# Three pair buffers, and channel halves for the first pair, in the opening statistics of a two-layer similarity kernel

## The chip, the cores and the metric

The kernel runs on one core of one Trainium2 chip. The metric is the device time of one execution in microseconds (us). Work is spread over five engines that run on their own and meet at semaphores: TensorE (PE, whose weight loads are shown as PEld), VectorE (DVE), ScalarE (ACT), GpSimd (POOL) and SyncE (SP), which here only issues transfers to the core's 16 DMA engines.

## The reference, cut to what matters

The input has the shape 2 x 256 x 256 x 384 (images, rows, columns, channels) in float32. Two equal layers run one after the other, each a group normalisation followed by a ratio of box sums that is added to the layer's input:

```python
def _gn(v, G=32, eps=1e-5):              # 12 channels in a group
    g = v.reshape(B_, H_, W_, G, C_ // G)
    m = jnp.mean(g, axis=(1, 2, 4), keepdims=True)
    s = jnp.var(g, axis=(1, 2, 4), keepdims=True)
    return ((g - m) / jnp.sqrt(s + eps)).reshape(v.shape)
# conv_ref(x), box sums of width 5 along W and 20 along C:
s = box_sum(x, 2, 5);  num = box_sum(s * s, 3, 20)
d = box_sum(box_sum(x * x, 2, 5), 3, 20)
ratio = nan_to_num(num / (d * norm), nan=1.0)
x = x + _L0_conv_ref(_gn(x))
x = x + _L1_conv_ref(_gn(x))
```

A mean and a variance of a group are taken over a whole image. So nothing of an image can be normalised before all of that image has been read once.

## The kernel before

The work has four phases, (layer, image) = (0, 0), (0, 1), (1, 0), (1, 1). An image has 32 tiles (`TILES`) of 8 rows; a tile is 3072 KB, in SBUF 128 partitions x 16 segments (`SEGS`) x 384 channels. In a phase TensorE forms the width sums and the channel sums for one pair of image rows after another, and the other engines centre, square, divide and add around it.

Ahead of phase 0 stands the opening: VectorE has to measure all 32 tiles of image 0, and no other engine has work meanwhile. The statistics of the other images are measured beside the phases, as a third user of VectorE's time (`measure_beside`, `measure_output`), and the change leaves them as they are.

In the opening two tiles are measured at a time, as a pair j of 0 to 15. `measure` issues 32 `bn_stats`, one for each group, over both tiles of the pair. A pair lies in `x_both` (even j) or `y_both` (odd j); each of its two tiles is loaded by a transfer of its own with its own semaphore (`in_landed[0..3]`). SyncE's program (`measure_loads`, L225) issues the four loads of pairs 0 and 1 at once. Then, for each pair that `tile_measured` counts as done, it issues the two loads of the pair that comes two later. So pair j + 2 can't be asked for before pair j is measured, and while pair j is being measured only pair j + 1 is on its way.

These loads take the image in an order in which a partition's part of a tile is one stretch of 24,576 bytes (16 x 384 x 4), which is allowed since a mean doesn't ask for an order. The last pair, 15, is loaded otherwise (L231): by channel halves. One transfer brings channels 0 to 191 of both tiles, the other the rest, in rows of 768 bytes (192 x 4), and VectorE measures 16 groups, sums them up, and does the same for the other 16. When pair 7 is measured, `opening_totals` (L643) sums up the first half of the image with 32 `bn_aggr`.

When pair 14 is measured, SyncE also issues the loads of the first two tiles of phase 0 (L237), in rows of 1,536 bytes. Behind the last `bn_aggr` come the short chain `ask_means` and `finish` (L680 to L723: VectorE and TensorE by turns, ScalarE for a logarithm and an exponential), and then the phases. `loads_before` tells POOL how many loads had gone into `x_both` before a phase.

Of the kernel before, what the change touches and what calls it, by code (L numbers as in the profile page):

```python
# [29 lines left out]
P = 128  # L30
# [21 lines left out]
def similarity_layers_kernel(nc, x, out):  # L52
# [9 lines left out]
    LAYERS = 2  # L62
    PHASES = [(layer, b) for layer in range(LAYERS) for b in range(B)]
    NP_ = len(PHASES)
    assert W == 2 * P and C == 3 * P and TILES % 4 == 0 and B == 2 and TILES >= 8

    SPLIT = TILES // 2
    CUT = GROUPS // 2
# [4 lines left out]
    BESIDE = TILES - UPFRONT  # L73
    BESIDE_SPLIT = (SPLIT - UPFRONT) // 2
    BESIDE_END = BESIDE // 2
    REACH = W_BOX // 2
    WN = P + REACH
    HALF_COL = [0, P - REACH]
# [12 lines left out]
    with ExitStack() as ctx:  # L91
        def sb(name, shape, dt=F32):
            return ctx.enter_context(nc.sbuf_tensor(name, shape, dt))
# [5 lines left out]
        y_both = sb("y_both", [P, 2 * SEGS, C])  # L99
        x_in = [x_both[:, i * SEGS:(i + 1) * SEGS, :] for i in range(2)]  # L100
        y_out = [y_both[:, i * SEGS:(i + 1) * SEGS, :] for i in range(2)]
        stat_tiles = [x_in[0], x_in[1], y_out[0], y_out[1]]
        stat_pairs = [x_both, y_both]
        centred = [sb(f"centred{i}", [P, PSEG, C]) for i in range(2)]
        square = [sb(f"square{i}", [P, PSEG, C]) for i in range(2)]
        sT = [sb(f"sT{i}", [P, KB, 2 * W]) for i in range(2)]
        tT = [sb(f"tT{i}", [P, KB, 2 * W]) for i in range(2)]
        recip = [sb(f"recip{i}", [P, PSEG, C]) for i in range(2)]
        with nc.sbuf_tensor("beside", [P, SEGS, C], F32) as beside:
            pass  # L110
        top = [sb(f"top{i}", [P, KB, 2 * W], BF16) for i in range(2)]
# [28 lines left out]

        in_landed = [sem(f"in_landed{i}") for i in range(4)]
        out_landed = [sem(f"out_landed{i}") for i in range(2)]
        ones_set = sem("ones_set")
        bands_cut = sem("bands_cut")
        bands_ready = sem("bands_ready")
# [64 lines left out]
        with nc.Block() as block:  # L210

            @block.sync
            def _(sp):

                view = tiles_of(x, 0)
                runs = x[0].rearrange("h w c -> (h w) c").rearrange("(t p s) c -> p t s c", p=P, s=SEGS)

                def measure_loads(i, lo):
                    for s in range(4):
                        if lo > 0 and s % 2 == 0:  # L220

                            sp.wait_ge(tile_measured, i * 2 + s // 2 - 1)
                        if lo == TILES // 4 - 1 and s >= 2:
                            continue
                        sp.dma_start(stat_tiles[s][:].unsqueeze(1), runs[:, bass.ds(i * 4 + s, 1), :, :]  # L225
                                     ).then_inc(in_landed[s], 16)
                looped(sp, TILES // 4, measure_loads, [0, TILES // 4 - 1])

                for part in range(2):
                    cs = slice(part * CUT * CG, (part + 1) * CUT * CG)  # L230
                    sp.dma_start(y_both[:, :, cs], view[:, (TILES - 2) * SEGS:TILES * SEGS, cs]  # L231
                                 ).then_inc(in_landed[2 + part], 16)

                for s in range(2):

                    sp.wait_ge(tile_measured, TILES // 2 - 1)
                    sp.dma_start(x_in[s][:], tiles_of(x, 0)[:, s * SEGS:(s + 1) * SEGS, :]  # L237
                                 ).then_inc(in_landed[s], 16)
                def load_beside(n):

                    sp.dma_start(beside[:], tiles_of(x, 1)[:, bass.ds((UPFRONT + n) * SEGS, SEGS), :]
                                 ).then_inc(beside_landed, 16)


                for s in range(UPFRONT):

                    sp.wait_ge(means_asked, 1)
                    sp.dma_start(y_out[s][:], tiles_of(x, 1)[:, s * SEGS:(s + 1) * SEGS, :]
                                 ).then_inc(in_landed[2 + s], 16)
                    if s == 0:  # L250
                        load_beside(0)

                sp.wait_ge(beside_done, 3)
                load_beside(1)
                for ph, (layer, b) in enumerate(PHASES):
                    src = tiles_of(source[layer], b)
                    dst = tiles_of(target[layer], b)
                    bodies = TILES // 2

                    def move_tiles(i, lo):  # L260
                        last = lo == bodies - 1
                        for s in range(2):
                            m = i * 2 + s
                            if last and s == 1 and ph == NP_ - 1:

                                for g in range(PAIRS):
                                    sp.wait_ge(rows_out, pairs_before(ph) + m * PAIRS + g + 1)
                                    sp.dma_start(dst[:, m * SEGS + g * PSEG:m * SEGS + (g + 1) * PSEG, :],
                                                 y_out[1][:, g * PSEG:(g + 1) * PSEG, :]
                                                 ).then_inc(out_landed[1], 16)  # L270
                                continue

                            sp.wait_ge(rows_out, pairs_before(ph) + (m + 1) * PAIRS)
                            if not last:
                                sp.dma_start(x_in[s][:], src[:, bass.ds((m + 2) * SEGS, SEGS), :]
                                             ).then_inc(in_landed[s], 16)
                            elif ph + 1 < NP_:
                                nl, nb = PHASES[ph + 1]
                                if nl > 0:

                                    for o in range(2):
                                        sp.wait_ge(out_landed[o], 16 * (TILES // 2) * (nb + 1))
                                sp.dma_start(x_in[s][:], tiles_of(source[nl], nb)[:, s * SEGS:(s + 1) * SEGS, :]
                                             ).then_inc(in_landed[s], 16)
                            sp.dma_start(dst[:, bass.ds(m * SEGS, SEGS), :], y_out[s][:]
                                         ).then_inc(out_landed[s], 16)
                            if ph == 0 and lo < BESIDE_END - 1:

                                sp.wait_ge(beside_done, (m + 2) * 3)
                                load_beside(m + 2)  # L290
                    looped(sp, bodies, move_tiles, [bodies - 1], [(BESIDE_END - 1, None)] if ph == 0 else [])

                for s in range(2):
                    sp.wait_ge(out_landed[s], 16 * ((TILES // 2) * NP_ + s * (PAIRS - 1)))


            def loads_before(ph):
                return TILES // 4 + ph * (TILES // 2)

            @block.gpsimd  # L300
            def _(pool):
# [303 lines left out]
            def _(dve):  # L605
# [38 lines left out]
                    link(last)  # L644


                def measure_two(base, i, s):

                    for o in range(2):
                        dve.wait_ge(in_landed[2 * s + o], (base + i + 1) * 16)  # L650
                    measure(stat_pairs[s], range(GROUPS), out_stats, i * 2 + s).then_inc(tile_measured, 1)

                for half in range(2):
                    with dve.Fori(0, SPLIT // 4 - half) as i:
                        for s in range(2):
                            measure_two(half * (SPLIT // 4), i, s)
                    if half == 0:
                        dve.wait_ge(tile_measured, SPLIT // 2)
                        opening_totals(0, range(GROUPS))

                measure_two(SPLIT // 4, SPLIT // 4 - 1, 0)
                for part in range(2):
                    groups = range(part * CUT, (part + 1) * CUT)
                    dve.wait_ge(in_landed[2 + part], TILES // 4 * 16)
                    link(measure(y_both, groups, out_stats, SPLIT // 2 - 1))
                    if part == 0:
                        dve.wait_ge(tile_measured, TILES // 2 - 1)
                    opening_totals(1, groups)


                dve.wait_ge(bands_cut, 2 * HALVES + KB + 1)
                for d in range(REACH):
# [92 lines left out]
                def measure_output(ph, i, lo, e, part):  # L765
# [6 lines left out]
                    if ph == 0 and lo == 0 and early:  # L772

                        if q == 0 or part == 0:
                            return
                        if q == 1:
                            dve.wait_ge(in_landed[3], (TILES // 4 + 1) * 16)

                        last = measure(y_out[1], range((q - 1) * chunk, GROUPS if q == 3 else q * chunk),
                                       beside_stats, 1)  # L780
                        if q == 3:
                            link(last)
                        return
# [57 lines left out]
                ask_means(0)  # L841
                finish(0)

                dve.wait_ge(in_landed[2], (TILES // 4 + 1) * 16)
                measure(y_out[0], range(GROUPS), beside_stats, 0).then_inc(tile_measured, 1)
                dve.wait_ge(tile_measured, TILES // 2)
                for ph in range(NP_):
# [49 lines left out]
```

## Time and profile before

| | us |
|---|---|
| median of three runs | 5876.69 |
| lowest and highest of the three | 5875.77, 5883.06 |
| the profiled execution's own time | 5877.14 |
| its span in the trace | 5875.4 |
| busy in the span: PE, PEld | 5516.0, 5489.9 |
| busy in the span: DVE, POOL, ACT | 4830.5, 4585.6, 4491.6 |

The span reaches from the first instruction of the program to the last one's end. Busy time of an engine is the union of its instructions' times. The granted clock of TensorE was 0.998 of its full speed in this execution. In the rows below a start is counted from the start of the span, and "idle before" is the time in which the engine did nothing, with the event that ended it.

### The profile page before, as it was taken

The page shows a single profiled execution, that of the slowest core. Times are in us where ns is not written, and L with a number is a line of the kernel's source. Part 1 is how long each engine was busy: PE and PEld are TensorE (multiplying, and loading weights), DVE is VectorE, ACT ScalarE, POOL GpSimd, SP SyncE. Part 2 cuts the span into 40 slices and gives each one's busy share as a digit, 9 for nine tenths or more (in the row PEclk, how much of TensorE's full clock was granted, in tenths as well). Part 3 has the DMA queues.
Part 4 walks back from the last instruction along what each step waited for, and adds up shares of the span by engine and source line. Part 5 has one row for each costly group of instructions (what it writes and reads, how often), then busy time and mean ns, then how long its engine had stood idle before and what let it go on. Part 6 is the DMA issues. An engine that isn't in the chain of part 4 may idle for free.

```text
span 5875.4 us, 145274 instructions
## 1 busy us (share of the span) xinstructions
PE 5516.0 (94%) x53804; PEld 5489.9 (93%) x53804; DVE 4830.5 (82%) x8140; ACT 4491.6 (76%) x6153; POOL 4585.6 (78%) x1427
## 2 busy tenths in 40 slices
PE   0099999999999999999999999999999999999999
PEld 0099999999999999999999999999999999999999
DVE  8988889988889999999999777777777777777776
ACT  0077777777877788878887788888888888888887
POOL 0056665566658899889998899999999999999998
PEclk9999999999999999999999999999999999999999
DMA  9965655566633444434344343444444443434343
GB/s 383 348 212 201 225 204 204 196 206 223 207 136 129 146 155 141 159 129 162 138 157 144 129 161 138 156 143 152 148 147 153 143 157 138 162 132 168 129 171 129
DMA packets 607136, 1007.81 MB, mean 172 GB/s; under 512 B 5168, under 2 KB 603184, under 8 KB 603184
## 3 DMA queue, kind: packets, MB, share of 16 engines
q1 hardware_dynamic: 607024, 1006.65, 48.1%
q14 instruction: 83, 0.68, 0.0%
q8 instruction: 29, 0.48, 0.0%
HBM read 603.98 MB, written 402.65 MB: 171 GB/s over the span
## 4 chain that ended last, share of the span: by engine, by line
PE 67%; DVE 4%; ACT 0%; issue 0%; POOLq 0%; POOL 0%; DVEq 0%; ACTq 0%
PE width_ps L527 35%; PE num_ps L555 18%; PE den_ps L564 14%; DVE recip L742 1%; DVE y_both L753 1%; DVE lane_mv L637 1%; DVE den_ps L735 1%; DVE out_stats L630 1%; PE den_ps L555 0%; DVE mid L728 0%; ACT recip L449 0%; DVE stat_two L684 0%; DVE beside_stats L630 0%; ACT top L430 0%; ACT recip L442 0%
## 5 line engine op out<-in xcount | busy, mean ns | idle before, releaser
L344 POOL TENSOR_TENSOR centred<-x_both,mean_row 128x1536 f32<-128x1536 f32 x512 | 1773.6, 3464 | 983.0 <-PE width_ps L527 690.4
L555 PE MATMUL num_ps<-band_c,sT 128*128 128x138 f32 (+2 forms) x12288 | 1811.6, 284 | 29.6 <-DVE y_both L753 29.2
L353 POOL TENSOR_TENSOR y_both<-x_both,y_both 128x1536 f32<-128x1536 f32 x512 | 1776.2, 3469 | 17.5 <-DVE y_both L753 17.5
L527 PE MATMUL width_ps<-band_wc,square 128*128 128x130 f32 x12288 | 1651.6, 277 | 17.0 <-DVE mid L728 12.5
L555 PEld LDWEIGHTS num_ps<-band_c,sT 128*128 128x128 f32 x12288 | 1609.0, 190 | 38.2 <-DVE y_both L753 13.6
L527 PE MATMUL width_ps<-band_w,centred 128*128 128x130 f32 x12288 | 1562.5, 276 | 0.0
L527 PEld LDWEIGHTS width_ps<-band_wc,square 128*128 128x128 f32 x12288 | 1507.1, 191 | 19.9 <-DVE mid L728 10.1
L527 PEld LDWEIGHTS width_ps<-band_w,centred 128*128 128x128 f32 x12288 | 1459.8, 191 | 0.4
L442 ACT ACTIVATE recip<-den_ps,bias_ln 128x768 f32<-128x768 f32 x1024 | 920.2, 899 | 644.8 <-PE den_ps L564 450.0
L735 DVE SCALAR_TENSOR_TENSOR den_ps<-den_ps,recip 128x768 f32<-128x768 f32 x1024 | 987.2, 964 | 499.2 <-ACT recip L449 472.6
L361 POOL TENSOR_TENSOR low<-mid 128x1536 bf16<-128x1536 f32 x384 | 1055.2, 2748 | 282.9 <-DVE mid L728 282.9
L433 ACT ACTIVATE sT<-width_ps,rstd_col 128x512 f32<-128x512 f32 x1536 | 1056.4, 688 | 208.9 <-PE width_ps L527 208.7
L728 DVE SCALAR_TENSOR_TENSOR mid<-width_ps,rvar_col,top 128x512 f32<-128x512 f32 x1152 | 860.9, 747 | 385.0 <-ACT top L430 383.9
L753 DVE SCALAR_TENSOR_TENSOR y_both<-num_ps,recip 128x768 f32<-128x768 f32 x1024 | 976.6, 954 | 67.1 <-DVE recip L742 2.0
L742 DVE SCALAR_TENSOR_TENSOR recip<-den_ps,recip 128x768 f32<-128x768 f32 x1024 | 974.5, 952 | 18.7
L449 ACT ACTIVATE recip<-recip,bias_exp 128x768 f32<-128x768 f32 x1024 | 952.6, 930 | 0.1
L430 ACT ACTIVATE top<-width_ps,rvar_col 128x512 bf16<-128x512 f32 x1152 | 791.8, 687 | 164.6 <-PE width_ps L527 110.7
L414 ACT ACTIVATE square<-centred 128x768 f32<-128x768 f32 x1024 | 853.9, 834 | 1.9 <-POOL centred L344 1.9
L564 PE MATMUL den_ps<-band_b,mid 128*128 128x138 bf16 (+2 forms) x4608 | 725.9, 225 | 0.0
L564 PE MATMUL den_ps<-band_b,top 128*128 128x138 bf16 (+2 forms) x4608 | 725.6, 225 | 0.0
L630 DVE BATCH_NORM_STATS2 out_stats<-y_both 128x192 f32 (+2 forms) x2304 | 696.4, 367 | 7.3 <-DMA y_both<-in_x_dram 6.8
L564 PE MATMUL den_ps<-band_b,low 128*128 128x138 bf16 (+2 forms) x4608 | 534.5, 225 | 0.0
(55 smaller groups left out, 2877.3 us busy)
## 6 DMA issues: line engine op xcount, KB each, us to landing
x_both<-in_x_dram SPq DMA_DIRECT2D x80, 3072.0 KB, 11.0
first_layer_out<-y_both SPq DMA_DIRECT2D x64, 3072.0 KB, 18.3
x_both<-first_layer_out SPq DMA_DIRECT2D x64, 3072.0 KB, 10.9
out_dram<-y_both SPq DMA_DIRECT2D x63, 3072.0 KB, 18.1
beside<-in_x_dram SPq DMA_DIRECT2D x30, 3072.0 KB, 10.9
y_both<-in_x_dram SPq DMA_DIRECT2D x18, 3072.0 KB, 16.8
out_dram<-y_both SPq DMA_DIRECT2D x4, 768.0 KB, 3.6
```

The lines of the kernel that those rows point to most:

```text
L344: nc.gpsimd.tensor_tensor(centred[e % 2][:], x_in[slot][:, g * PSEG:(g + 1) * PSEG, :], mean_row[ph % 2][:].unsqueeze(1).to_broadcast([P, ...
L353: nc.gpsimd.tensor_tensor(y_out[slot][:, g * PSEG:(g + 1) * PSEG, :], x_in[slot][:, g * PSEG:(g + 1) * PSEG, :], y_out[slot][:, g * PSEG:( ...
L361: nc.gpsimd.tensor_tensor(low[par][:], mid[par][:], top_half(mid[par]), ALU.subtract).then_inc(low_cut, 1)
L433: nc.scalar.activation(sT[par][:, k, :], src, ACT.Square, scale=rstd_col[ph][:, k:k + 1]).then_inc(width_taken, 1)
L442: nc.scalar.activation(recip[par][:, 2 * h:2 * h + 2, :], den_ps[h][:, :, 0:C], ACT.Ln, bias=bias_ln[:], scale=LN_SCALE).then_inc(log_done, 1)
L449: nc.scalar.activation(both, both, ACT.Exp, bias=bias_exp[:], scale=-1.0).then_inc(recip_done, 1)
L527: last = nc.tensor.matmul(bank[:, at:at + WN], data[:, r * 2 + j, P * k:P * (k + 1)], band[:, j, :], start=(r == 0 and j == 0), stop=(r == ...
L555: last = nc.tensor.matmul(bank[:, lo:hi], data[:, k, at:at + P], band_c[k][:], start=(k == 0), stop=(k == KB - 1), skip_group_check=True)
L564: last = nc.tensor.matmul(bank[:, lo:hi], thirds[n][:, k, at:at + P], band_b[k][:], start=(n == 0 and k == 0), stop=(n == 2 and k == KB - ...
L735: nc.vector.scalar_tensor_tensor(near, near, TINY, recip[par][:, 2 * h:2 * h + 2, :], ALU.add, ALU.mult).then_inc(near_done, 1)
L742: nc.vector.scalar_tensor_tensor(both, den_ps[h][:, :, 0:C], 2.0, both, ALU.subtract, ALU.mult).then_inc(den_used, 1)
L753: nc.vector.scalar_tensor_tensor(y_out[slot][:, at:at + 2, :], num_ps[:, :, 0:C], TINY, recip[e % 2][:, 2 * h:2 * h + 2, :], ALU.add, ALU.mult
```

## The change

The opening statistics use three buffers of two tiles, in turn: pair j goes into buffer j % 3 of `y_both`, `spare_pair`, `x_both`. `spare_pair` is a new name for memory that is otherwise idle in the opening: it lies where `centred`, `square`, `sT` and `tT` are later, 49,152 bytes of each partition, and ends where they end. SyncE issues the loads of pairs 0, 1 and 2 at once and those of pair j when pair j - 3 is measured. Pair 0 is loaded and measured by channel halves, as the last pair already was. Pair 14 still lies in `x_both` and pair 15 in `y_both`. The loops of the opening on SyncE and on VectorE are written out in full, and the counts that later waits compare with are adapted (`X_USES` 5, `Y_USES` 6).

```diff
+    X_USES = (TILES // 2 - 1) // 3
+    Y_USES = X_USES + 1
...
-        stat_tiles = [x_in[0], x_in[1], y_out[0], y_out[1]]
-        stat_pairs = [x_both, y_both]
+        with nc.sbuf_tensor("spare_pair", [P, 2 * SEGS, C], F32) as spare_pair:
+            pass
...
+        stat_pairs = [y_both, spare_pair, x_both]
...
+        spare_landed = [sem(f"spare_landed{i}") for i in range(2)]
+        stat_landed = [in_landed[2:4], spare_landed, in_landed[0:2]]
...
-                def measure_loads(i, lo):
-                    for s in range(4):
-                        if lo > 0 and s % 2 == 0:
-
-                            sp.wait_ge(tile_measured, i * 2 + s // 2 - 1)
...
+                for j in range(TILES // 2):
+                    if j >= 3:
+
+                        sp.wait_ge(tile_measured, j - 2)
+                    for part in range(2):
+                        if j in (0, TILES // 2 - 1):
+                            cs = slice(part * CUT * CG, (part + 1) * CUT * CG)
+                            sp.dma_start(stat_pairs[j % 3][:, :, cs], view[:, j * 2 * SEGS:(j + 1) * 2 * SEGS, cs]
+                                         ).then_inc(stat_landed[j % 3][part], 16)
+                        else:
+                            m = j * 2 + part
+                            sp.dma_start(stat_pairs[j % 3][:, part * SEGS:(part + 1) * SEGS, :].unsqueeze(1),
+                                         runs[:, m:m + 1, :, :]).then_inc(stat_landed[j % 3][part], 16)
...
-                return TILES // 4 + ph * (TILES // 2)
+                return X_USES + ph * (TILES // 2)
...
+                def measure_halves(j):
+
+                    for part in range(2):
+                        groups = range(part * CUT, (part + 1) * CUT)
+                        dve.wait_ge(stat_landed[j % 3][part], (j // 3 + 1) * 16)
+                        last = measure(stat_pairs[j % 3], groups, out_stats, j % (SPLIT // 2))
+                        if j == TILES // 2 - 1:
+                            link(last)
+                            if part == 0:
+                                dve.wait_ge(tile_measured, TILES // 2 - 1)
+                            opening_totals(1, groups)
+                    return last
+
+                measure_halves(0).then_inc(tile_measured, 1)
+                for j in range(1, TILES // 2 - 1):
+                    for part in range(2):
+                        dve.wait_ge(stat_landed[j % 3][part], (j // 3 + 1) * 16)
+                    measure(stat_pairs[j % 3], range(GROUPS), out_stats, j % (SPLIT // 2)).then_inc(tile_measured, 1)
+                    if j == SPLIT // 2 - 1:
+                        dve.wait_ge(tile_measured, SPLIT // 2)
+                        opening_totals(0, range(GROUPS))
+                measure_halves(TILES // 2 - 1)
```

On SyncE, at the start of its program, this stood before, with the loop that the branch closes:

```order
L225 DMA x_both<-in_x_dram 128x6144 x2
L225 DMA y_both<-in_x_dram 128x6144 x2
L201 UNCONDITIONAL_BRANCH
L201 ISA
L225 ISA [waits tile_measured]
L225 DMA x_both<-in_x_dram 128x6144
L225 ISA
L225 DMA x_both<-in_x_dram 128x6144
L225 ISA [waits tile_measured]
L225 DMA y_both<-in_x_dram 128x6144
```

And this stands at the same place of SyncE's program of the changed kernel:

```order
L230 DMA y_both<-in_x_dram 128x32x192 x2
L234 DMA spare_pair<-in_x_dram 128x6144 x2
L234 DMA x_both<-in_x_dram 128x6144 x2
L234 DMA y_both<-in_x_dram 128x6144 [waits tile_measured]
L234 DMA y_both<-in_x_dram 128x6144
L234 DMA spare_pair<-in_x_dram 128x6144 [waits tile_measured]
```

Six loads now stand ahead of the first wait in place of four, and the first two of them are the halves of pair 0, which are in rows of 192 channels.

On VectorE, behind the fourteen `memset` of its program, each `bn_stats` of a looped pair had a register instruction (ISA) of its own before. A piece of it, at the end of pair 0's and the start of pair 1's:

```order
L630 ISA
L630 BN_STATS out_stats<-x_both 128x6
L630 ISA [waits in_landed3,in_landed2]
L630 BN_STATS out_stats<-y_both 128x6
L630 ISA
```

The same stretch of VectorE's program of the changed kernel, from pair 0 to pair 3:

```order
L633 BN_STATS out_stats<-y_both 128x6 [waits in_landed2]
L633 BN_STATS out_stats<-y_both 128x6 x15
L633 BN_STATS out_stats<-y_both 128x6 [waits in_landed3]
L633 BN_STATS out_stats<-y_both 128x6 x15
L633 BN_STATS out_stats<-spare_pair 128x6 [waits spare_landed1,spare_landed0]
L633 BN_STATS out_stats<-spare_pair 128x6 x31
L633 BN_STATS out_stats<-x_both 128x6 [waits in_landed1,in_landed0]
L633 BN_STATS out_stats<-x_both 128x6 x31
```

The first 16 `bn_stats` now wait for one half alone and the next 16 for the other, there are as many of them as before, and the register instructions are gone.

## Rows read from the trace of the kernel before

**Rows 1.** The page's slices: busy tenths of an engine in 40 equal slices

```profile
PE   0099999999999999999999999999999999999999
DVE  8988889988889999999999777777777777777776
```

**Rows 2.** Waits in the opening: who waited for whom, us, times, longest

```profile
PE den_ps L499 <- DVE stat_two L684: 291.2, 1, 291.2
DVE out_stats L630 <- DMA x_both<-in_x_dram: 28.6, 7, 16.2
DVE out_stats L630 <- DMA y_both<-in_x_dram: 6.8, 5, 1.7
```

**Rows 3.** VectorE's timeline, opening: start, us, line, form, idle before

```profile
18.53 14.81 DVE L630 BATCH_NORM_STATS2 out_stats<-x_both 128x384 f32 x32 [16.24 <-DMA x_both<-in_x_dram]
33.30 14.81 DVE L630 BATCH_NORM_STATS2 out_stats<-y_both 128x384 f32 x32
51.37 14.81 DVE L630 BATCH_NORM_STATS2 out_stats<-x_both 128x384 f32 x32 [3.26 <-DMA x_both<-in_x_dram]
67.22 14.81 DVE L630 BATCH_NORM_STATS2 out_stats<-y_both 128x384 f32 x32 [1.05 <-DMA y_both<-in_x_dram]
...
147.53 7.51 DVE L643 BATCH_NORM_AGGREGATE lane_mv<-out_stats 128x2 f32<-128x48 f32 x32
155.45 14.81 DVE L630 BATCH_NORM_STATS2 out_stats<-x_both 128x384 f32 x32 [0.42 <-DVE lane_mv L643]
...
267.49 7.44 DVE L630 BATCH_NORM_STATS2 out_stats<-y_both 128x6 f32<-128x384 f32 x16
...
286.31 3.82 DVE L643 BATCH_NORM_AGGREGATE lane_mv<-out_stats 128x2 f32<-128x48 f32 x16
290.17 0.34 DVE L674 TENSOR_SCALAR band_wc<-band_w 128x1 f32<-128x1 f32 x4
```

**Rows 4.** SyncE's loads issued at 0.8 to 2.2: issue, then landing

```profile
L225 SPq DMA_DIRECT2D x_both<-in_x_dram x2: 402/412/421, 0.8 to 1.3; - x2
DMA to landing us min/median/max: 10.2/13.6/17.0
...
L225 SPq DMA_DIRECT2D y_both<-in_x_dram x2: 424/499/574, 1.7 to 2.2; - x2
DMA to landing us min/median/max: 23.9/27.4/30.9
```

**Rows 5.** The same for the loads issued at 33.5 and at 48.3

```profile
L225 SPq DMA_DIRECT2D x_both<-in_x_dram x2: 338/343/348, 33.5 to 34.1; - x2
DMA to landing us min/median/max: 10.3/13.7/17.1
...
L225 SPq DMA_DIRECT2D y_both<-in_x_dram x2: 332/332/333, 48.3 to 48.8; - x2
DMA to landing us min/median/max: 11.4/14.8/18.2
```

**Rows 6.** The same for L231, pair 15's halves in rows of 768 bytes

```profile
L231 SPq DMA_DIRECT2D y_both<-in_x_dram x2: 383/3962/7541, 251.5 to 252.0; - x2
DMA to landing us min/median/max: 13.0/17.6/22.2
```

**Rows 7.** The same for L237, phase 0's tiles in rows of 1,536 bytes

```profile
L237 SPq DMA_DIRECT2D x_both<-in_x_dram x2: 1433/3555/5677, 267.6 to 269.1; - x2
DMA to landing us min/median/max: 15.0/18.4/21.8
```

**Rows 8.** Windows: stretch, busy us of engines, granted clock, DMA share, GB/s

```profile
5.00:10.00 5.00, 0.00 (x0) 0.00 (x0) 0.00 (x0) 0.00 (x0) 1.70 (x6) 1.00 1.03 442
10.00:18.00 8.00, 0.00 (x0) 0.00 (x0) 0.00 (x0) 0.00 (x0) 0.00 (x0) 1.00 0.99 427
51.00:98.00 47.00, 0.00 (x0) 0.00 (x0) 43.81 (x95) 0.00 (x0) 0.00 (x0) 1.00 0.95 395
```

**Rows 9.** Line L707 in all phases: duration ns min, median, max

```profile
L707 DVE TENSOR_SCALAR stat_tmp<-stat_tmp x4: 180/182/2627, 294.4 to 3333.6; 128x32 f32<-128x32 f32 x4
```

More of the change, by code:

```diff
@@ L64, in similarity_layers_kernel @@
     NP_ = len(PHASES)
-    assert W == 2 * P and C == 3 * P and TILES % 4 == 0 and B == 2 and TILES >= 8
+    assert W == 2 * P and C == 3 * P and TILES // 2 % 3 == 1 and B == 2 and TILES >= 8
     SPLIT = TILES // 2
@@ L216, in _ @@
                 runs = x[0].rearrange("h w c -> (h w) c").rearrange("(t p s) c -> p t s c", p=P, s=SEGS)
-                def measure_loads(i, lo):
-                    for s in range(4):
-                        if lo > 0 and s % 2 == 0:
-                            sp.wait_ge(tile_measured, i * 2 + s // 2 - 1)
[L223 to L232, printed above, removed]
+                for j in range(TILES // 2):
[10 more added lines that the diff above has]
+                                         runs[:, m:m + 1, :, :]).then_inc(stat_landed[j % 3][part], 16)
                 for s in range(2):
@@ L644, in opening_totals @@
                     link(last)
[L647 to L657, printed above, removed]
+                def measure_halves(j):
[15 more added lines that the diff above has]
+                    if j == SPLIT // 2 - 1:
                         dve.wait_ge(tile_measured, SPLIT // 2)
                         opening_totals(0, range(GROUPS))
[L661 to L668, printed above, removed]
+                measure_halves(TILES // 2 - 1)
                 dve.wait_ge(bands_cut, 2 * HALVES + KB + 1)
@@ L776, in measure_output @@
                         if q == 1:
-                            dve.wait_ge(in_landed[3], (TILES // 4 + 1) * 16)
+                            dve.wait_ge(in_landed[3], (Y_USES + 1) * 16)
                         last = measure(y_out[1], range((q - 1) * chunk, GROUPS if q == 3 else q * chunk),
@@ L842, in _ @@
                 finish(0)
-                dve.wait_ge(in_landed[2], (TILES // 4 + 1) * 16)
+                dve.wait_ge(in_landed[2], (Y_USES + 1) * 16)
                 measure(y_out[0], range(GROUPS), beside_stats, 0).then_inc(tile_measured, 1)
```

## The prediction

> **What bounds the kernel now.** First the page's slices [rows 1]: TensorE is at 9 tenths or more in 38 slices and idle in the first two. From the start of phase 0 on TensorE sets the pace and VectorE has room; in the opening it is the other way round. The waits say what TensorE stands for there: 291.2 us for `stat_two`, the first thing that VectorE makes from the finished statistics [rows 2]. Nothing else runs meanwhile, so a microsecond saved before 290.17, where the last `bn_aggr` has ended [rows 3], starts everything behind it a microsecond earlier.
>
> VectorE's timeline shows what fills these 290 us [rows 3]. From 18.53 to 33.30 it measures a pair without a pause: 14.77 us. Sixteen pairs make 236.3 us. The sums after pair 7 take 155.45 - 147.53 = 7.9 us, those at the end some 2 x 3.8. Together 251.8. The rest is waiting for loads: 28.6 + 6.8 = 35.4 us in twelve waits [rows 2]. 16.2 of them are the wait for the first pair; 19.2 stand between pairs, 3.26 ahead of pair 2, 1.05 ahead of pair 3, and so on.
>
> Why does it wait between pairs, if the transfers are fast enough? The landings tell. The four loads issued at 0.8 to 2.2 land at 11.0, 18.3, 25.6 and 33.1 [rows 4]. So a load into an idle queue takes 10.2 us, and each one queued behind it only 7.3 to 7.5 more. The first thus has some 10.2 - 7.3 = 2.9 us of start. Two queued loads, a pair, need 14.6 to 14.8 us, which is VectorE's own 14.77. But the loads issued at 33.5 found the queue empty since 33.1 and landed at 43.8 and 51.2 [rows 5]: 18 us for a pair. The next, issued at 48.3, when the queue had 2.9 us of work left, landed at 59.7 and 67.0 [rows 5]: 8.5 + 7.3 = 15.8 us after 51.2. The queue runs nearly dry once in every pair, because the next pair may be asked for only when VectorE has finished one. From 51 to 98 us the transfers move 395 GB/s, from 5 to 18 us, with the queue full, 442 and 427 [rows 8].
>
> **The change, part by part.**
>
> Third buffer. The loads of pair j + 3 are issued when pair j is measured; then pairs j + 1 and j + 2 are landed, moving or queued. The queue does not run dry. I take 14.7 us for a pair, from the loads queued deep [rows 4]. The bounds are 14.6 and the 15.8 of a shallow queue [rows 5].
>
> Pair 0 by halves. The half loads of pair 15 show the price: issued at 251.5 and 252.0, landed at 264.5 and 274.2 [rows 6]. That is 9.7 us for a half (of both tiles, again 3072 KB) in place of 7.3. The first half goes into an idle queue at 0.8 and should land at 0.8 + 2.9 + 9.7 = 13.4, the second at 23.1. VectorE begins 0.2 after a landing (18.53 against 18.3), measures 16 groups in 7.4 us from 13.6 to 21.0, waits, and measures the others from 23.3 to 30.7. Before, pair 0 was done at 33.30. Issuing the second half holds SyncE for 7.5 us [rows 6], so the loads of pairs 1 and 2 are issued at about 9 to 11; the queue has work until 23.1, so this costs nothing.
>
> Now the price: pair 1 is behind these slower halves. Its tiles land at 30.4 and 37.8, and VectorE starts it at 38.0 where before it started at 33.30. Starting early buys nothing that is kept, since pair 1 is 4.7 us later. Pair 2 lands at 37.8 + 14.7 = 52.5 and is started at 52.8, against 51.37 before. Until here the change is 1.4 us behind.
>
> The Trainium skill (DMA: Bandwidth & Descriptors, Specifications) puts the size from which a transfer runs at line rate at 512 B, so 768 bytes would cost what 24,576 do. Pair 1 would then land at 0.8 + 2.9 + 4 x 7.3 = 32.9, and the gain be 4.9 us larger. The trace disagrees with its 9.7 against 7.3, though with other loads ahead and behind it; the row is taken, and 7.3 is its lower bound.
>
> From pair 1 on. VectorE needs 14.77 a pair and the queue 14.7, so VectorE sets the pace, barely. Pairs 1 to 7 end at 38.0 + 7 x 14.77 = 141.4. The 7.9 of sums bring it to 149.3, and in this time the loads get ahead by as much. Pairs 8 to 14 end at 252.7. The tail from the start of pair 15 to 290.17 was 290.17 - 267.49 = 22.7 [rows 3] with both halves there in time; now they are asked for one pair earlier and the queue has more to spare. So the statistics end at 275.4 in place of 290.17: **14.8 us earlier**.
>
> What else moves. There are as many `bn_stats` and `bn_aggr` as before. The register instructions of the loops go; they cost nothing, as pairs measured in the loop follow one another in 14.77 and the straight-line half of pair 15 takes 7.44 [rows 3]. The loads of phase 0's first two tiles leave, as before, when pair 14 is measured, 22.7 us ahead of the end, and took 15.0 and 21.8 to land [rows 7] while pair 15's second half was still moving; now nothing is moving, so they are no later. `spare_pair` is last used by pair 13, and the first write into `centred` waits for the means anyway. Behind 290 us the instructions and buffers are the same.
>
> The sum: 5877.14 - 14.8 = 5862.3 for the profiled execution. Its own time is 0.4 above the median of the three runs, by which it would be 5861.9. I say **5862.0**. A measurement of this kernel can tell about 0.2% from no change, 11.8 us, so the gain is 3 us above that bound.
>
> **The rivals.**
>
> *The shallow queue's price stays.* The 8.5 us between 51.2 and 59.7 [rows 5] could be a price of each new issue and not of its lateness. For it: it is so wherever a pair is asked for in the middle of another's transfer. Against it: the third load at the start was issued 16.6 us ahead of its turn and landed 7.3 after the second [rows 4]. Then pair j lands at 37.8 + 15.8 (j - 1), pair 7 at 132.6; its measuring and the sums end at 155.5; pair 8 is there by then, and so is each pair up to 14 (243.2, against 244.1 on VectorE), which ends at 258.9. Plus 22.7 makes 281.6, a gain of 8.6: 5868.5. Chance 0.12.
>
> *Straight code stalls.* One instruction of VectorE's stands out: L707 took 2627 ns once, in the opening, and some 182 otherwise [rows 9]. The trace does not say why; it may have waited for its code. The change writes 512 `bn_stats` out, each run once, and shifts all of VectorE's later code. Each such stall in the opening costs 2.4 us, with nothing to hide it; two to four make 5867 to 5872. On the other side L707's own may vanish, which would give up to 2 us more. Against it: the straight-line parts around 267.49 show no such pause. Chance 0.08.
>
> *The rate falls under a full queue, slower than before.* The opening is then bound by transfers from end to end. The point from which this decides: before, pair 14 was started 14.77 before 267.49, at 252.7. If its load lands later than 252.5, the change loses. That is (252.5 - 23.1) / 14 = 16.4 us a pair, or 6.29 MB (2 x 3072 KB) / 16.4 = 384 GB/s. The nearest rows are those of L237: 282.6 and 290.9, so 8.3 for a tile in rows of 1,536 bytes [rows 7]. At 16.6 a pair, pair 14 lands at 255.5 and the opening ends 3 us later than before: 5880. It takes 17.2 a pair to be slower by 0.2%. Against it stand the 442 and 427 GB/s, though over 13 us only [rows 8]. Chance 0.05.
>
> The Trainium skill (DMA: Bandwidth & Descriptors, Where 436 GB/s comes from) has a rule for this rival: between HBM and SBUF the HBM side binds at about 358 GB/s a core. At that rate, an estimate from this page, a pair takes 17.6 us and the time would be some 5894. The trace already moves 395 over 47 us with pauses in it, so I give the rule no more than that chance.
>
> *Something behind the opening gives the gain back*, a shifted load or loop: I see no place for it, chance 0.05.
>
> **How the numbers follow.** The forecast has 0.70, with a range of its own of 5857 (halves at 7.3) to 5865 (pairs at 15.0 in place of 14.7 for the first seven, 2 us, and 1 us of scatter). The shallow queue reaches to 5868.5 and two stalls to 5867. I take 5857 to 5870; about 1.5 in 10 is outside. Faster by over 0.2%, below 5864.9: nearly all of the forecast's 0.70 and a little of stalls with one stall only, 0.72. Within 0.2%: the shallow queue, most of the stalls, half of the falling rate and most of what gives the gain back, 0.24. Slower by over 0.2%: 0.04.
>
> **What the profile of the changed kernel would show.** VectorE's first `bn_stats` at 13.6, a wait of some 2 us ahead of the second half, a long one of about 7 ahead of pair 1 to 38, and then waits of under 0.3 us for each pair; pair 2 at about 52.8, and the last `bn_aggr` ended at 275.4. Loads of 24,576-byte stretches land 7.3 to 7.5 after one another across pairs too. Where they land 8.5 apart at each new pair, the first rival is right. Pauses inside a pair, with its load long landed, would be the stalls. TensorE's first wait should be 276.4, and its waits behind it unchanged. The prediction is wrong if the rate across pairs is not that of the first four loads, or if the halves of pair 0 do not take 9.7 at the start, where VectorE is idle.

## The result, and the profile after

| | median us | runs | ratio to before, 95% interval |
|---|---|---|---|
| before | 5877.02 | 10 | |
| changed | 5863.55 | 10 | 0.9976, 0.9968 to 0.9985 |

The change makes the kernel 13.5 us faster, 0.23%. The forecast was 5862.0, in a range of 5857 to 5870. One of the ten runs of the changed kernel, 20152 us at a granted clock of 0.444 of full speed, is left out of the ratio.

The profiled execution has a span of 5863.4 us, 12.0 under that of before. The page, and the waits of its opening:

```profile
span 5863.4 us, 144735 instructions
...
PE 5512.5 (94%) x53804; PEld 5486.7 (94%) x53804; DVE 4830.7 (82%) x8140; ACT 4491.7 (77%) x6153; POOL 4585.5 (78%) x1427
```

```profile
PE den_ps L502 <- DVE stat_two L686: 275.7, 1, 275.7
...
DVE out_stats L633 <- DMA y_both<-in_x_dram: 13.6, 3, 11.0
DVE out_stats L633 <- DMA spare_pair<-in_x_dram: 7.2, 1, 7.2
...
DVE out_stats L633 <- DMA x_both<-in_x_dram: 0.2, 1, 0.2
```

TensorE now waits 275.7 us for the statistics in place of 291.2 [rows 2]. VectorE's waits for loads are 13.6 + 7.2 + 0.2 = 21.0 in place of 35.4, and they lie elsewhere. VectorE's timeline in the opening, which answers to [rows 3]:

```profile
13.25 7.46 DVE L633 BATCH_NORM_STATS2 out_stats<-y_both 128x6 f32<-128x384 f32 x16 [10.96 <-DMA y_both<-in_x_dram]
22.86 7.45 DVE L633 BATCH_NORM_STATS2 out_stats<-y_both 128x6 f32<-128x384 f32 x16 [2.16 <-DMA y_both<-in_x_dram]
37.55 14.81 DVE L633 BATCH_NORM_STATS2 out_stats<-spare_pair 128x6 f32<-128x384 f32 x32 [7.24 <-DMA spare_pair<-in_x_dram]
52.51 14.81 DVE L633 BATCH_NORM_STATS2 out_stats<-x_both 128x6 f32<-128x384 f32 x32 [0.15 <-DMA x_both<-in_x_dram]
67.23 14.79 DVE L633 BATCH_NORM_STATS2 out_stats<-y_both 128x6 f32<-128x384 f32 x32
...
111.92 14.81 DVE L633 BATCH_NORM_STATS2 out_stats<-y_both 128x6 f32<-128x384 f32 x32 [0.48 <-DMA y_both<-in_x_dram]
...
141.47 7.51 DVE L646 BATCH_NORM_AGGREGATE lane_mv<-out_stats 128x2 f32<-128x48 f32 x32
...
251.97 7.44 DVE L633 BATCH_NORM_STATS2 out_stats<-y_both 128x6 f32<-128x384 f32 x16
...
274.65 0.34 DVE L676 TENSOR_SCALAR band_wc<-band_w 128x1 f32<-128x1 f32 x4
```

Three waits at the start (10.96, 2.16, 7.24), then one of 0.15 and one of 0.48. The statistics end at 274.65, 15.5 us before 290.17. The landings of pair 0's halves, and the transfer rate (stretch, busy us, clock, DMA share, GB/s) in the window behind them:

```profile
L230 SPq DMA_DIRECT2D y_both<-in_x_dram x1: 436/436/436, 0.8 to 0.8; - x1
DMA to landing us min/median/max: 12.4/12.4/12.4
...
L230 SPq DMA_DIRECT2D y_both<-in_x_dram x1: 7163/7163/7163, 1.3 to 1.3; - x1
DMA to landing us min/median/max: 21.5/21.5/21.5
```

```profile
24.00:105.00 81.00, 0.00 (x0) 0.00 (x0) 73.61 (x161) 0.00 (x0) 0.00 (x0) 1.00 1.00 430
105.00:220.00 115.00, 0.00 (x0) 0.00 (x0) 114.45 (x266) 0.00 (x0) 0.00 (x0) 1.00 1.00 430
```

The halves land at 13.2 and 22.8, 9.6 us apart. Behind them the queue moves 430 GB/s for nearly 200 us without a gap, where it moved 395 between 51 and 98 before [rows 8]. This is the whole of the change's work, and it did what it says.

But 15.5 us were won in the opening and 12.0 arrive at the end of this execution. The sums of `beside_stats`, all in phase 0, mark where the rest goes; their first and last start, in the kernel before and in the changed one:

```profile
L637 DVE BATCH_NORM_AGGREGATE lane_mv<-beside_stats x64: 528/530/574, 903.5 to 1696.5; 128x2 f32<-128x96 f32 x64
```

```profile
L640 DVE BATCH_NORM_AGGREGATE lane_mv<-beside_stats x64: 526/529/577, 885.4 to 1684.8; 128x2 f32<-128x96 f32 x64
```

At 903.5 the changed kernel is 18.1 us ahead, 2.6 more than at the opening's end. At 1696.5 it is 11.7 ahead. So 6.4 us are lost between the two, and there is no edit there. VectorE's waits ended by "issue" (the engine waited for nothing that the view shows), the whole of them, before and after:

```profile
DVE beside_stats L630 <- issue: 13.6, 8, 1.8
```

```profile
DVE beside_stats L633 <- issue: 7.2, 4, 1.9
DVE den_ps L737 <- issue: 5.1, 4, 1.4
```

Before, 8 pauses of 1.7 us; after, 4 of 1.8 and 4 of 1.3, the latter at a place where there was none. One of them, in VectorE's timeline of the changed kernel:

```profile
1384.71 1.13 DVE L633 BATCH_NORM_STATS2 out_stats<-y_both 128x192 f32 x4
1387.42 0.88 DVE L633 BATCH_NORM_STATS2 beside_stats<-beside 128x192 f32 x3 [1.58 <-issue]
1389.71 0.97 DVE L737 SCALAR_TENSOR_TENSOR den_ps<-den_ps,recip 128x768 f32<-128x768 f32 x1 [1.41 <-issue]
```

The first is at the start of a round of a loop (8 pairs of image rows), the second a few instructions on. Phase 0 has two such loops on VectorE, of four or five rounds. In the trace before, four pauses lie in rounds of the first loop (between 300 and 850 us) and four in those of the second (between 1130 and 1550). In the changed kernel the first loop has none and the second has all eight. That asks for a cause, and the experiments have two threads: what each half of the change is worth, and what makes these pauses.

### The profile page after: what moved, and what is told of

The parts are those of the page before. It is cut to its first block, busy times and chain, and to the rows that moved or that the text cites. A ratio compares the mean times of both kernels' runs of the same rounds, so it can differ in the third digit from the quotient of the medians.

```text
span 5863.4 us, 144735 instructions
## 1 busy us (share of the span) xinstructions
PE 5512.5 (94%) x53804; PEld 5486.7 (94%) x53804; DVE 4830.7 (82%) x8140; ACT 4491.7 (77%) x6153; POOL 4585.5 (78%) x1427
## 4 chain that ended last, share of the span: by engine, by line
PE 67%; DVE 4%; issue 0%; ACT 0%; POOLq 0%; POOL 0%; DVEq 0%; ACTq 0%
PE width_ps L530 35%; PE num_ps L558 18%; PE den_ps L567 14%; DVE recip L744 1%; DVE y_both L755 1%; DVE lane_mv L640 1%; DVE den_ps L737 1%; DVE out_stats L633 1%; PE den_ps L558 0%; DVE mid L730 0%; ACT recip L452 0%; DVE beside_stats L633 0%; ACT top L433 0%; ACT recip L445 0%; DVE stat_two L686 0%
## 5 line engine op out<-in xcount | busy, mean ns | idle before, releaser
L737 DVE SCALAR_TENSOR_TENSOR den_ps<-den_ps,recip 128x768 f32<-128x768 f32 x1024 | 987.4, 964 | 507.7 <-ACT recip L452 475.9
L633 DVE BATCH_NORM_STATS2 out_stats<-y_both 128x192 f32 (+2 forms) x2240 | 666.8, 362 | 14.1 <-DMA y_both<-in_x_dram 13.6
```

The lines of the kernel that those rows point to most:

```text
L737: nc.vector.scalar_tensor_tensor(near, near, TINY, recip[par][:, 2 * h:2 * h + 2, :], ALU.add, ALU.mult).then_inc(near_done, 1)
```

## The experiments

Two theories on the opening. **Queue**: the gain comes from the queue that never runs dry, and the halves of pair 0 cost more than they bring, since pair 1 stands behind them. **Early start**: the halves bring the gain. Two on the pauses. **Place** (A): where a loop stands in VectorE's program decides. **Moment** (B): the phases start at another moment of the loads. The change writes out VectorE's opening, and all later instructions stand 191 places further on (counted in the built programs, before they are compiled).

### The third buffer alone

```diff
-                        if j in (0, TILES // 2 - 1):
+                        if j == TILES // 2 - 1:
...
-                measure_halves(0).then_inc(tile_measured, 1)
-                for j in range(1, TILES // 2 - 1):
+                for j in range(TILES // 2 - 1):
```

> The changed kernel with three buffers, but pair 0 loaded as two whole tiles in stretches of 24,576 bytes and measured at once, as the pairs behind it. Theory of the prediction (a transfer queue that never runs dry, 7.3 us a tile, and halves of 9.6): pair 0 lands at 18.3 and is measured from 18.5, pair 1 lands at 33.0 and is measured from 33.3 in place of 37.55, all else follows at 14.7 a pair, and the last sums end at about 270.4, 4.2 us before those of the changed kernel (274.6). Time about 5859.5. Rival (the halves are what gives the gain, by starting VectorE at 13.25): the statistics end later than 274.6 and the time is 5867 or more.

Measured: 5859.15 us (6 runs), ratio 0.9968 (0.9956 to 0.9980). VectorE's timeline:

```profile
18.31 14.81 DVE L633 BATCH_NORM_STATS2 out_stats<-y_both 128x6 f32<-128x384 f32 x32 [16.03 <-DMA y_both<-in_x_dram]
33.04 14.79 DVE L633 BATCH_NORM_STATS2 out_stats<-spare_pair 128x6 f32<-128x384 f32 x32
47.76 14.81 DVE L633 BATCH_NORM_STATS2 out_stats<-x_both 128x6 f32<-128x384 f32 x32
...
269.92 0.34 DVE L675 TENSOR_SCALAR band_wc<-band_w 128x1 f32<-128x1 f32 x4
```

VectorE starts 5.1 us later than with the halves and is through 4.7 us earlier: the price was there for pair 1. The queue theory holds, and this is the first version that beats both kernels. The intervals of the two ratios overlap; what tells them apart are the medians, 4.4 us apart, the single times (the highest of these six is 5860.23, the lowest of the changed kernel 5861.31), and the traces.

### The halves alone

The written-out loops with two buffers, pair 0 by halves:

```diff
-        stat_pairs = [y_both, spare_pair, x_both]
+        stat_pairs = [x_both, y_both]
...
-                    if j >= 3:
-                        sp.wait_ge(tile_measured, j - 2)
+                    if j >= 2:
+                        sp.wait_ge(tile_measured, j - 1)
```

> Two buffers as before, but pair 0 by channel halves, and the loops of the opening written out. Theory: pair 1, queued behind two slow halves, lands at 37.5 where it was measured from 33.3 before; the later pairs wait 1.0 to 1.8 us each as before, since each is asked for only when the last but one is measured. The last sums end at 292 to 294, later than before (290.1), and the time is 5879 to 5883. Rival (the early start is worth 5 us and is kept): the sums end near 285 and the time is 5872.

Measured: 5882.88 us (11 runs), ratio 1.0009 (1.0000 to 1.0018), 5.8 above before. VectorE's timeline:

```profile
37.61 14.81 DVE L630 BATCH_NORM_STATS2 out_stats<-y_both 128x6 f32<-128x384 f32 x32 [7.24 <-DMA y_both<-in_x_dram]
52.58 14.81 DVE L630 BATCH_NORM_STATS2 out_stats<-x_both 128x6 f32<-128x384 f32 x32 [0.16 <-DMA x_both<-in_x_dram]
70.02 14.81 DVE L630 BATCH_NORM_STATS2 out_stats<-y_both 128x6 f32<-128x384 f32 x32 [2.64 <-DMA y_both<-in_x_dram]
...
294.26 0.34 DVE L673 TENSOR_SCALAR band_wc<-band_w 128x1 f32<-128x1 f32 x4
```

The opening ends 4.1 us later than in the trace of before, as expected, but with two buffers that end moves from one execution to another: three traces with the looped opening of before have it at 290.17, 294.74 and 296.88 (the latter two are of kernels below). With three buffers it does not: 274.65, 274.31 and 274.31 with the halves, 269.92 and 269.82 with whole tiles. So the change has one part worth some 20 us in the opening (290.17 to 269.92) and one that costs 4 to 5 us with three buffers. With two buffers the median is 5.8 us worse, and some of that is due to the pauses, which lie here as in the changed kernel; what the halves cost there in the opening isn't shown apart.

### The kernel before, moved by 191 places

```diff
                 nc.vector.memset(over_p[:], 0.5 / P)
+                for n in range(191):
+                    nc.vector.memset(rstd_row[:, n:n + 1], 0.0)
```

> The kernel before with 191 one-column fills of a scratch row on VectorE, put in its wait for the first load, so that all of its later instructions stand 191 places further on, as in the changed kernel; nothing else. Theory A (where the loops of phase 0 stand in VectorE's program decides how long it pauses in each round for want of instructions): the opening ends at 290.1 as before, the idle time that ends with an issue goes from 8 pauses of 1.6 us ahead of L630's beside_stats to the changed kernel's pattern (4 of those and 4 of 1.3 us ahead of the first den_ps operation), and the time is 1 to 4 us above that of the kernel before, about 5880. Theory B (the changed kernel loses 3.5 us behind the opening because its phases start at another moment of the loads): pauses and time as before, 5877.

Measured: 5878.41 us (11 runs), ratio 1.0002 (0.9993 to 1.0011). The time alone decides nothing, since this execution's opening ended late (294.74, where 290.1 was expected). Its sums of `beside_stats`, and its pauses:

```profile
L639 DVE BATCH_NORM_AGGREGATE lane_mv<-beside_stats x64: 528/530/573, 905.9 to 1700.7; 128x2 f32<-128x96 f32 x64
```

```profile
DVE beside_stats L632 <- issue: 8.4, 8, 1.8
```

The four pauses of the first loop are gone, though nothing in this kernel but the place changed, and from the opening's end to the first sums it takes 611.2 us (905.9 - 294.7) where before it took 613.3 and the changed kernel 610.8. All eight lie in the second loop, as theory A says. The second pause of a round is only 0.4 us where 1.3 were expected, and it comes ahead of the next `bn_stats` and not of L737's operation, so the pattern is not the changed kernel's to the letter: the second loop loses 1.8 us against before (794.8 in place of 793.0), not 6.4. Theory B is out for the first loop. And the fills themselves show, in VectorE's timeline, what is being waited for:

```profile
2.20 0.85 DVE L623 MEMSET rstd_row<- 128x1 f32 x52
3.45 3.64 DVE L623 MEMSET rstd_row<- 128x1 f32 x128 [0.40 <-issue]
9.05 0.35 DVE L623 MEMSET rstd_row<- 128x1 f32 x11 [1.97 <-issue]
```

In a run of 191 equal instructions VectorE pauses after the 52nd and then after exactly 128 more. Its program comes in pieces of 128 instructions.

The compiled programs explain where the second pause stands. The compiler drops jumps to the instruction that follows, so there (counted without labels) the loops of the changed kernel stand 193 places on and those of this kernel 191. With the pieces cut where the fills paused, 8 instructions of the second loop lie ahead of a cut in the changed kernel and 10 in this one. The second pauses stand exactly there: ahead of L737's operation, the 9th instruction of the round, and of the `bn_stats` that is the 11th. Why the one takes 1.3 us and the other 0.4 isn't shown.

### The changed kernel, moved on to 256 places

65 such fills in the changed kernel, 191 + 65 = 256 places in the built program (258 in the compiled one).

> The changed kernel with 65 such fills in VectorE's first wait, so that its later instructions stand 256 places behind those of the kernel before. Theory A, with a period of 256 places or a divisor of it: the pauses of phase 0 are those of the kernel before again (8 of 1.6 us ahead of beside_stats, none ahead of den_ps), the opening ends at 274.6, and the profiled span is some 3.5 us under the changed kernel's 5863.4, near 5860. Theory B: span and pauses as in the changed kernel.

Measured: 5859.90 us (6 runs, 5859.44 to 5860.30), ratio 0.9970 (0.9958 to 0.9982); span 5858.2, where near 5860 was expected. The opening ends at 274.31, and the pauses:

```profile
DVE beside_stats L635 <- issue: 13.7, 8, 1.9
```

This is the pattern of before, 8 pauses at the start of a round. From the first to the last sum of `beside_stats` it is 792.9 us (888.0 to 1680.9), as before. 65 instructions that do nothing useful win 3.7 us: theory A.

### Without any pause

A loop of phase 0 is 343 instructions long (counted in the built program). Over four pieces of 128 it pauses, over three it should not. From the place of the second pause both loops lie over three pieces when they stand 7 to 14 places further on than in the changed kernel. Three kernels: whole tiles with 9 fills, the changed kernel with 10, the kernel before with 73.

> The version with three buffers and pair 0 as whole tiles, with 9 one-column fills in VectorE's first wait, so that both long loops of phase 0 (343 instructions each) stand 9 places further on. Theory A, made sharper by the runs so far: VectorE's program is cut at every 128th place, and a loop that lies over three such pieces runs without pauses, one that lies over four pauses once in a round, at its start, or twice where only its first few instructions lie in the first piece. By the place of the second pause in the changed kernel both loops lie over three pieces from 7 to 14 places further on. Then no idle time of VectorE in phase 0 ends with an issue, and against the kernel with whole tiles (5859.15) the second loop gives back 6.7 us and the 0.7 us that a single pause costs in each of four rounds: about 5850. Rival B: the pauses do not follow the place, and the time is 5859.

> The changed kernel with 10 fills, so that its loops stand where those of the version with whole tiles and 9 fills do. Theory A: no pauses in phase 0, opening ended at 274.6 as in the changed kernel, about 5854. Rival B: as the changed kernel, 5863.

> The kernel before with 73 fills: its loops then stand 128 places ahead of those of the two other kernels of this call. Theory A with a period of 128: no pauses in phase 0, opening as before (290 to 295, as the fills made the first loads land later once), and the time is 5.5 us under that of the kernel before for an opening of 290, about 5871.5, and up to 5876 for a later one. With a period of 256 instead: pauses stay, 5877 or more.

| | median us (runs) | ratio | first and last sum of `beside_stats` |
|---|---|---|---|
| whole tiles, 9 fills | 5850.09 (5) | 0.9951, 0.9937 to 0.9964 | 880.4, 1670.9 |
| changed, 10 fills | 5854.05 (5) | 0.9959, 0.9945 to 0.9972 | 884.8, 1675.2 |
| before, 73 fills | 5871.95 (11) | 0.9989, 0.9980 to 0.9998 | 907.8, 1698.2 |

All three came out within 0.5 us of what was expected. VectorE's longest waits from 300 to 1600 us in the first of them; no line ended by "issue" is left behind the opening in any of the three:

```profile
DVE den_ps L738 <- ACT recip L452: 112.9, 129, 2.5
DVE y_both L756 <- DVE recip L745: 2.0, 10, 0.2
```

From the first to the last sum it is 790.5, 790.4 and 790.4 us, 2.6 less than before and 9.0 less than in the changed kernel. The profiled execution of the third is the slowest of its eleven (5877.22, opening ended at 296.88), so its own time stands above the median. The first, 5850.09, is the best version found: 28 us under the kernel before, 13.5 under the changed one.

### What all nine traces say of the pauses

The profile also counts the packets of the queues that bring instructions. Those of q14 are 8 KB each, which is 128 instructions of 64 bytes. The line of the whole execution, for the kernel before, the changed one, and whole tiles with 9 fills:

```profile
q14 instruction: 83, 0.68, 0.0%
```

```profile
q14 instruction: 65, 0.53, 0.0%
```

```profile
q14 instruction: 45, 0.37, 0.0%
```

Where each of the two loops starts within a piece (0 to 127, counted without labels in the compiled programs, from the cut that the fills show), how often it pauses in all (8 is twice a round), and these packets. A loop of 343 fits into three pieces when it starts at 41 or less:

| | starts | pauses | q14 packets |
|---|---|---|---|
| before | 90, 55 | 4, 4 | 83 |
| changed | 27, 120 | 0, 8 | 65 |
| whole tiles | 28, 121 | 0, 8 | 66 |
| halves alone | 27, 120 | 0, 8 | 65 |
| before, 191 fills | 25, 118 | 0, 8 | 65 |
| changed, 65 fills | 92, 57 | 4, 4 | 86 |
| whole tiles, 9 fills | 37, 2 | 0, 0 | 45 |
| changed, 10 fills | 37, 2 | 0, 0 | 45 |
| before, 73 fills | 35, 0 | 0, 0 | 44 |

Each loop that pauses costs some 20 packets more, 5 for each of its four returns to the start: from 1130 to 1560 us, where the second loop runs, the changed kernel has 22 of them and whole tiles with 9 fills 2. So in a pausing loop the pieces are brought anew in each round, and in a loop over three pieces they aren't.

## Why the prediction was right, point by point

*What bounds the opening, and the third buffer.* Right. The queue ran at 430 GB/s throughout and VectorE set the pace from pair 2 on. The opening ended 0.7 us before the forecast 275.4: pair 1 was started 0.45 earlier, and the pairs follow one another in 14.72 (52.51 to 67.23) where 14.77 was reckoned; the wait of 0.48 took most of the latter back. The loads of pairs 1 and 2 were forecast to be issued at about 9 to 11; the issue of pair 1's first held SyncE for 9.55 us, and pair 2's left at 18.6. The queue still had the second half to move until 22.8, so this cost nothing.

*The halves.* Right in mechanism and size: landings forecast at 13.4 and 23.1, measured at 13.2 and 22.8; pair 1 forecast at 38.0, measured 37.55; pair 2 at 52.8 against 52.51. That they cost 4.7 us in all was in the working ("pair 1 is 4.7 us later") but the step to a better version was not made. The 512 B rule of the Trainium skill (DMA: Bandwidth & Descriptors, Specifications) would have had them land 7.3 apart; with VectorE idle and no other load ahead of the two, rows of 768 bytes still took 9.6. The measurement decides against the rule for this size.

*The sum.* 14.8 forecast, 15.5 measured in the opening.

*"Behind 290 us the instructions and buffers are the same."* True of the instructions and wrong as a step to the time: of the 15.5 only 12.0 arrived in the profiled execution and 13.5 in the medians. The last rival, a shifted loop that gives the gain back, is what happened in part, and the prediction gave it 0.05 and no price since it saw "no place for it": 2.6 us won in the first loop, 6.4 lost in the second. The second rival had the code that shifts too, but priced it as stalls in the opening, where no new one came: L709, the former L707 [rows 9], took 2.63 us as before, and the 512 written-out `bn_stats` ran without a pause. The cost came in a loop some 900 us behind the opening, through its place. It was visible: the trace of before had 13.6 us of waits ended by "issue" at the starts of rounds, and the prediction did not look there. That these pauses follow the place is shown by nine kernels, and that they are the fetching of instructions by the packets, some 20 fewer for each loop that stops pausing. The total still came out near the forecast since the loss behind the opening is small, 3.5 us, and the opening itself was 0.7 better than forecast.

*The other rivals.* The shallow queue's price is refuted for deep queues: VectorE waits only once behind pair 2, for 0.48 us, and with two buffers the waits of 2.64 and the like are back. The falling rate, 384 GB/s, is refuted: 430 for 196 us. The 358 GB/s of the HBM side that the Trainium skill gives (DMA: Bandwidth & Descriptors, Where 436 GB/s comes from) did not bind this core, which ran alone.

## What to carry to other kernels

Where a stage lives on transfers, look at when each load is asked for against the landing of the one ahead of it: here a queue that was fed 3 us before it ran dry lost over a microsecond each time (8.5 in place of 7.3), and one more buffer won nearly all of it back. A strided first load starts the work earlier but delays all that queue behind it; count to the second wait, not the first. And an edit that lengthens an engine's program moves its loops: compare the waits ended by "issue" before and after, and try a few idle instructions ahead of the loops before taking or refusing an edit worth a few microseconds.

## What was not expected of the hardware

A loop of 343 instructions on VectorE ran without a pause when it lay over three pieces of 128 instructions, and paused 1.6 to 1.9 us a round when it lay over four; where only its first 7 to 10 instructions lay in the first piece, a second pause of 0.4 to 1.4 us came behind them. The price for the kernel was some 0.7 us a round for one pause (about 2.6 for a loop) and 1.1 (second pause of 0.4) to 2.2 us (of 1.3) for two. The Trainium skill (Runtime: NRT & Kernel Launch, Instruction fetch mechanics) says that a taken branch whose target lies outside the two pages that are held forces a fetch before execution goes on. The pauses at the start of a round agree with that. But it gives pages of 256 instructions, where the runs show steps of 128 and packets of 8 KB, and a loop that lay over three such pieces ran without a pause.

With the queue always full, a tile in 24,576-byte stretches lands some 7.3 us behind the one before, but now and then some 8.3 (8.4 below). The loads of two pairs in a row in the changed kernel:

```profile
L234 SPq DMA_DIRECT2D x_both<-in_x_dram x2: 328/380/433, 67.3 to 67.7; - x2
DMA to landing us min/median/max: 21.6/25.1/28.5
...
L234 SPq DMA_DIRECT2D y_both<-in_x_dram x2: 328/380/433, 82.1 to 82.4; - x2
DMA to landing us min/median/max: 22.5/25.9/29.4
```

These land at 88.9 and 96.2 and at 104.6 and 111.8: 7.3, 8.4, 7.2. The late one is VectorE's only wait behind pair 2, the 0.48 us at 111.92. Its cause is open.
